# Three PSUM banks for the row-maximum scores, two for the transposed scores, in the experts' attention of a language-model tower

## The reference, cut to what matters

```
h = _ln(jax.nn.relu(x @ ew1 + eb1) @ ew2 + eb2, eg, ebeta)
qkv = h @ aiw + aib
q, k, v = jnp.split(qkv, 3, axis=-1)
...
attn = jax.nn.softmax(jnp.einsum('bhqd,bhkd->bhqk', q, k) * SCALE, axis=-1)
o = jnp.einsum('bhqk,bhkd->bhqd', attn, v).transpose(0, 2, 1, 3).reshape(h.shape)
h = o @ aow + aob
```

## Time and profile before

| what | value |
|---|---|
| median of three runs | 5243.91 us |
| the profiled execution's own time | 5246.02 us |
| its span, first to last instruction | 5244.2 us |
| TensorE busy | 5011.5 us, 96% |
| VectorE busy | 4117.5 us, 79% |
| ScalarE busy | 2392.4 us, 46% |
| GpSimd busy | 1150.5 us, 22% |
| mean granted TensorE clock | 0.978 |

### The profile page before, as it was taken

The page is one execution under the profiler, slowest core; times in us unless marked ns, Lnnn a source line. Parts: engine busy times, 40 slices in busy tenths (PEclk is TensorE's granted clock), DMA queues, the critical chain, the costliest instruction groups (busy, mean ns, idle before and its releaser), DMA issues. The chain is left out here.

```text
span 5244.2 us, 258310 instructions
## 1 busy us (share of the span) xinstructions
PE 5011.5 (96%) x108704; PEld 3523.4 (67%) x108704; DVE 4117.5 (79%) x19249; ACT 2392.4 (46%) x8343; POOL 1150.5 (22%) x5133
## 2 busy tenths in 40 slices
PE   7989799999999996999999999999999999998995
PEld 4656333333333335999999999899999999984442
DVE  3857666666666648999999999999999999991225
ACT  2734565555555535444444444444444444442332
POOL 0000011111111102333333333333333333330000
PEclk9989899999999998999999999999999999999997
DMA  0034554544545431111111011111111011102210
GB/s 15 1 99 144 135 90 89 112 101 84 126 89 121 91 134 49 37 31 27 41 25 41 17 41 25 41 29 29 41 25 41 17 41 25 41 1 89 72 42 13
DMA packets 378787, 302.27 MB, mean 58 GB/s; under 512 B 146105, under 2 KB 357561, under 8 KB 372954
## 3 DMA queue, kind: packets, MB, share of 16 engines
q1 hardware_dynamic: 378382, 298.20, 23.9%
HBM read 179.14 MB, written 119.01 MB: 57 GB/s over the span
## 5 line engine op out<-in xcount | busy, mean ns | idle before, releaser
L1439 PE MATMUL bank<-lparts,lstate 128*32 128x256 bf16 x98304 | 2697.0, 273 | 55.9 <-PEq L1382 46.8
L1439 PEld LDWEIGHTS bank<-lparts,lstate 128*32 128x32 bf16 x98304 | 2457.4, 97 | 296.1 <-issue 47.6
L1450 DVE STREAM_TRANSPOSE ltz<-bank 128x256 f32<-128x256 f32 x2048 | 920.7, 450 | 9.5 <-PE bank L1439 4.0
L1514 ACT ACTIVATE ltc<-lgc 128x16 f32<-128x16 f32 x2049 | 443.1, 216 | 1030.4 <-DVE lgc L1471 1030.4
L1528 POOL TENSOR_TENSOR wh<-lgate,ltc 128x16 f32<-128x16 f32 x2052 | 471.1, 230 | 1798.6 <-ACT ltc L1514 1727.9
L1255 ACT ACTIVATE wh<-bank 128x512 f32<-128x512 f32 x1024 | 550.0, 600 | 481.9 <-PE bank L1042 481.5
L1167 DVE TENSOR_REDUCE bnegmax<-bank 128x1 f32<-128x512 f32 x1024 | 654.0, 682 | 129.0 <-PE bank L1024 128.5
L1509 ACT ACTIVATE lgate<-lz 128x48 f32<-128x48 f32 x2048 | 498.9, 244 | 521.4 <-DVE lz L1461 521.4
L1535 POOL COPY ltz<-wh 128x64 f32<-128x64 f32 x2048 | 604.1, 295 | 0.0
L1457 DVE TENSOR_TENSOR lhalf<-ltz 128x128 f32<-128x128 f32 x2048 | 581.9, 284 | 10.2 <-POOL ltz L1535 6.1
L1104 PE MATMUL bank<-xT,bw 128*128 128x512 f32 x1024 | 489.4, 602 | 2.7 <-DVE bzs L1188 1.9
(11 more groups left out here) (208 smaller groups left out, 4294.2 us busy)
## 6 DMA issues: line engine op xcount, KB each, us to landing
zx<-bzs SPq DMA_DIRECT2D x32, 2048.0 KB, 7.3
wh<-zx SPq DMA_DIRECT2D x64, 1024.0 KB, 7.4
qk<-eparts SPq DMA_DIRECT2D x96, 256.0 KB, 2.8
bqp<-qk SPq DMA_DIRECT2D x192, 128.0 KB, 4.8
bkp<-qk SPq DMA_DIRECT2D x192, 128.0 KB, 8.1
hs<-wh SPq DMA_DIRECT2D x32, 512.0 KB, 5.8
cmemT<-hs SPq DMA_DIRECT2D x32, 512.0 KB, 4.5
vx<-evx SPq DMA_DIRECT2D x16, 544.0 KB, 4.2
```

The costliest lines, as they stand in the source:

```text
L1439: last = nc.tensor.matmul(bank[x][32 * q:32 * q + 32, 0:256], top[:, x, e, k].rearrange("p m r -> p (m r)"), parts[:, way, g, k, n, e, q], ...
L1450: nc.vector.transpose(tz[:, x].rearrange("p (n w) -> p n w", w=SLOT)[:, :, 0:32], bank[x][:, 0:256].rearrange("p (n c) -> p n c", n=BLOCKS ...
L1514: nc.scalar.activation(tc[:, x], gc[:, x, 1], ACT.Tanh).then_inc(tanhed[x], 1)
```

## The change

Scores take banks 0, 1 and 4 in turn, transposed scores banks 2 and 3. The waits follow: `score` now waits for the maximum of three scores before, `score_t` for the exponent of two transposed scores before. In TensorE's step the third score moves ahead of place A and the third transposed score behind it. The order of VectorE, ScalarE, GpSimd and the DMA queue stays as it is.

```diff
+        SCORE_BANKS = (0, 1, 4)
...
-                    if BT * j + qt >= 2:
-                        pe.wait_ge(maxed, BT * j + qt - 1)
-                    nc.tensor.matmul(bank[qt % 2][:], qp[0:KROWS, h, qt * P:(qt + 1) * P], kp[0:KROWS, h],
+                    if BT * j + qt >= 3:
+                        pe.wait_ge(maxed, BT * j + qt - 2)
+                    nc.tensor.matmul(bank[SCORE_BANKS[(BT * j + qt) % 3]][:], qp[0:KROWS, h, qt * P:(qt + 1) * P], kp[0:KROWS, h],
...
-                    if n >= 3:
-                        pe.wait_ge(exped, n - 2)
-                    nc.tensor.matmul(bank[2 + n % 3][:], kp[:, h, kt * P:(kt + 1) * P], qp[:, h], start=True,
+                    if n >= 2:
+                        pe.wait_ge(exped, n - 1)
+                    nc.tensor.matmul(bank[2 + n % 2][:], kp[:, h, kt * P:(kt + 1) * P], qp[:, h], start=True,
...
                     if 2 <= j < HEADS + 2:
-                        for kt in range(3):
+                        for kt in range(2):
                             score_t(j - 2, kt)
+                    if j < HEADS:
+                        score(j, 2)
                     if at == 1:
...
-                    if j < HEADS:
-                        score(j, 2)
                     if 2 <= j < HEADS + 2:
-                        score_t(j - 2, 3)
+                        for kt in range(2, BT):
+                            score_t(j - 2, kt)
                     if j < HEADS:
                         score(j, 3)
...
-                    nc.vector.tensor_reduce(negmax[:, j % NH, qt:qt + 1], bank[qt % 2][:], AX.X, ALU.max,
+                    nc.vector.tensor_reduce(negmax[:, j % NH, qt:qt + 1], bank[SCORE_BANKS[(BT * j + qt) % 3]][:], AX.X, ALU.max,
...
-                    nc.scalar.activation(pT[:, j % RING, kt], bank[2 + n % 3][:], ACT.Exp).then_inc(exped, 1)
+                    nc.scalar.activation(pT[:, j % RING, kt], bank[2 + n % 2][:], ACT.Exp).then_inc(exped, 1)
```

## The result

The changed kernel takes 5258.35 us, the kernel before 5245.05 us (medians of 10 runs each): a ratio of 1.0025, 95% interval 1.0016 to 1.0035, so 8 to 18 us slower. The forecast was 5254.3 us, +10.4 us or 0.20%, in a range of 5249 to 5262. Single executions of one kernel spread over 5 to 8 us (5242.98 to 5248.22 before, 5253.8 to 5261.31 after), so the trace tells more than the medians. The profiled execution took 5257.88 us, 11.9 us over that of before, and from the first score of head 0 to that of head 255 it took 1905.02 - 597.76 = 1307.26 us, against 1296.08 before: 11.2 us lie in this stage.

A forecast was written before the change was run, and what follows sets the result against it. TensorE, 96% busy, was taken as the bound, losing time where matmuls start late on waits. Terms: -4.3 + 7.3 + 6.3 + 1.2 + 0 - 0.1 = +10.4 us, giving a median of 5254.3 us, range 5249 to 5262.

The forecast's parts named there:

- Ramp steps: Early steps without product cover: third and fourth transposed scores wait for exponents, +0.45 us a step, +7.3 us with step 6.
- third transposed score's wait: Sign in ramp steps: its weights wait about 0.35 us for the first exponent.
- Gap steps: Steps without product cover: fourth transposed score waits for the second exponent, +0.42 us in 15 steps, +6.3 us.
- Double steps: Double product steps: second score no longer waits for the previous step's last maximum, 72 x 0.06 = -4.3 us.
- Turn steps: Four small transposes cover too little of the second exponent: 30 x 0.04 = +1.2 us.
- Third and fourth step: The third loses some 0.15 us, the fourth's projection waits for ScalarE anyway: taken as 0, between -1.5 and +2.2 us.
- First steps: Half-clock start: head 2 about 1 us forward, then losses at exponents; -0.1 us, between -1 and +1.
- step 6: Begins late at its rows, so +0.5 us is counted for it with the ramp.
- "clock" rival: More unused TensorE time in the ramp drops the clock to half: +33 us, to 5288; chance 0.02.
- first rival: First transposed score after single steps waits for turned maxima once keep_rows ends over 0.1 us later: 5263; chance 0.10.
- second rival: Deeper score ring lets the first score's weight load pass under values: -10.6 us, to 5243.7; chance 0.12.
- sign of being wrong: Ramp steps staying at 3.3 us, keep_rows as releaser in product steps, or the clock leaving 1.00 after 620 us.

The follow-up runs named there:

- repeated run: The changed kernel run again with no edit: 5258.53 us, ratio 1.0022 to the kernel before.
- rings alone: Changed kernel's three score banks and two transposed-score banks, but TensorE's order of the kernel before: 5392.97 us, ratio 1.0276 to the kernel before.
- bank given back: Changed kernel with bank 7 as third transposed-score bank in the ramp and for each gap step's third transposed score: 5242.69 us, ratio 0.9989 to the kernel before.
- order alone: Changed kernel's TensorE order, but two score and three transposed-score banks as in the kernel before: 5343.81 us, ratio 1.0182 to the kernel before.
- two delayed runs: Changed kernel with two or six small extra ScalarE copies ahead of keep_rows in product steps: 5262.27 and 5297.41 us, ratios 1.0028 and 1.0098 to before.
- run with two copies: Changed kernel with two small extra copies on ScalarE ahead of keep_rows in every product step: 5262.27 us, ratio 1.0028 to the kernel before.

## Why the prediction was right, point by point

The forecast of +10.4 us stands against +13.3 (8 to 18) by the medians and +11.2 us by the stage's own length. The mechanism is the forecast one, costed by kinds of steps whose durations repeat. The closeness of the total is in part luck. From step 7 on the stage grew by 9.3 us, in the repeated run too, where the forecast's terms give 9.95. The steps up to there took 1.8 us more than before in the first profile and 1.4 us less in the repeated one, where the forecast had +0.4. So the stage's own length is +11.2 us in one execution and +7.9 in the other. Term by term:

- **Ramp steps**: forecast 3.72 us, measured 3.71; 15 x 0.446 = 6.7 us, as forecast (15 x 0.45). Only the third transposed score's wait was put a little low as a sign: its matmul starts 0.42 us later than with a third bank (+1.51 instead of +1.09), where "about 0.35" was said. That the shorter ring does it is shown by the run with a third bank there (3.23) and by the rings alone (3.71).
- **Gap steps**: forecast +0.42, measured 4.20 - 3.78 = 0.42; 6.4 us. Shown by the bank given back (3.72).
- **Double steps**: forecast -0.06, measured 6.551 - 6.615 = -0.064, 72 times, 4.6 us. The wait of the second score is gone from the trace, and the run of the order alone, with two score banks, has it again. The 86 single steps became 0.003 us shorter each, another 0.3 us.
- **Turn steps**: forecast +0.04, 1.2 us; measured +0.04, 1.1 us.
- **Third and fourth step**: taken as 0; the third grew by 0.15 us, the fourth shrank by as much, 10.86 us together before and after.
- **First steps**: mis-sized. Head 2 starts 1.0 us earlier relative to head 0 (597.76 to 602.58, against 597.99 to 603.81), as worked out. But step 6 was to cost +0.5 us and cost +2.0, since the clock rose 5 us later; in the repeated run, with the clock up before it, it cost +0.6. This is the "clock" rival in a small form that the prediction did not have: not a fall, but a later rise after the idle stretch. The repeated run shows that the rise differs between executions. Whether the change makes a late rise likelier stays open: three of the four profiles with these first steps have it late, against a single profile of the kernel before.
- **The first rival's threshold**: the spare time of 0.1 us, from "can take its weights up to 0.1 us earlier", was half of what there was. The load may come as late as the matmul itself, so the margin was 0.2 us, as the two delayed runs show. `keep_rows` ended at +0.20 us of the next step, where the prediction had +0.19, and it holds up none of the product steps that have scores.
- **The second rival** did not occur: the load of the first score sits idle the same 0.85 us with three score banks, in ramp and double steps alike.
- **The clock** stayed at 1.00 from 625 us to the end of the stage with 0.7 us of waits in each ramp step. The prediction had named as a sign of being wrong a clock that leaves 1.00 after 620 us; read to the letter, the 5 us at the low level up to 625 us are such a sign, but the clock had not fallen there, it had not risen yet. The warning of the Trainium skill (TensorE: Matmul & The Clock Gate, A second HAM failure mode: psum-queue depth-cycling) has no counterpart in this stage: its granted clock is 1.00 over the 1300 us from 625 to 1925.

The table of waits moved as said: exponent to transposed score +19 us (forecast 15 to 25). The rule of the Trainium skill (Perfetto Trace Analysis, Optimization Strategy) about repeating gaps finds the place and names one remedy, more buffers: with one more bank the ramp step goes from 3.71 to 3.23 us. The exchange of two matmuls, with the banks as they are, takes it to 3.50.

The terms add up: 6.7 + 6.4 - 4.6 - 0.3 + 1.1 + 0 + 1.8 (the steps up to 7) = 11.1 us, against 11.2 for the stage. The remaining 2 us between medians and stage are within the spread of single executions.

## What to carry to other kernels

When buffers are moved from one ring to another, list the kinds of steps and ask in each what covers the wait of the ring that shrinks; the steps with an empty place A, though only 31 of 256 here, decided the sign. Ring depth and order of issue are one choice: either alone cost 1.8 to 2.8%, both together 0.25%. And before spending a buffer, look for a ready instruction that stands behind the waiting one in the same queue: here one exchanged pair returned all that the change had lost.

## What was not expected of the hardware

- A weight load that comes late costs its matmul almost nothing of its own 0.10 us: load and matmul are recorded at the same start (645.22 and 645.22; 1298.25 and 1298.26). In the run with two copies the load came 0.19 us later than in the changed kernel and the matmul 0.005 us.
- Small copies in a row on ScalarE cost less than their records: six of 128x16, each recorded with 0.21 us, took 0.74 us together, since they start 0.11 us apart; two delayed what followed by 0.2 us.
- The low clock after TensorE's idle stretch of 25 us ended at very different places in two executions of one kernel, at 625 us and at 612 us of the span. That is worth 3 us of the kernel's time, a quarter of the whole effect that was measured here.
